# Cross-attention without the loop over pairs, with the product of probabilities and values taken for four tiles at a time

## What is computed

```python
q = proj(norm(x), Wq, bq); k = proj(context, Wk, bk); v = proj(context, Wv, bv)
scores = clip(einsum('bhsd,bhtd->bhst', q, k) / 4, -50, 50)
scores = clip(where(attend, scores, -10000.0), -50, 50)
probs = softmax(scores); probs = probs / (probs.sum(-1) + 1e-08)
ctx = einsum('bhst,bhtd->bhsd', probs, v)
delta = clip(residual_scale, 0, 0.3) * (ctx @ Wo.T + bo)
x = x + layernorm(delta) * ln_gamma + ln_beta
```

## Time and profile before

| what | value |
|---|---|
| median of 3 runs | 1797.5 us (1793.64 to 1798.63) |
| profiled execution, its own time | 1795.94 us |
| its span, first to last instruction | 1794.1 us |
| PE busy | 1594.6 us, 89% |
| PE weight loads busy | 1341.1 us, 75% |
| DVE busy | 1454.5 us, 81% |
| ACT busy | 1117.9 us, 62% |
| POOL busy | 734.8 us, 41% |
| granted PE clock, mean | 0.946 |

### The profile page before, as it was taken

One profiled execution on the slowest core, in us unless ns is written; L12 is line 12 of the kernel. 1 busy time (PEld: TensorE's weight loads), 2 busy tenths in 40 slices (PEclk: granted clock), 3 DMA queues, 4 the chain that ended last, 5 costly groups with the idle time before them and its releaser, 6 DMA issues. The chain is left out here.

```text
span 1794.1 us, 48379 instructions
## 1 busy us (share of the span) xinstructions
PE 1594.6 (89%) x18290; PEld 1341.1 (75%) x18290; DVE 1454.5 (81%) x2513; ACT 1117.9 (62%) x2155; POOL 734.8 (41%) x743
## 2 busy tenths in 40 slices
PE   5899999998739999999999999999999999999464
PEld 5888888886528878787887787877877878788233
DVE  3788877875467898888888988888889888898698
ACT  3566555664337776676676666766766667677463
POOL 1565555553163443443343434433434344343133
PEclk9999999998769999999999999999999999999678
DMA  6000000000221111111111111111111111110001
GB/s 183 1 1 2 2 1 1 1 0 1 85 79 47 48 48 39 45 47 48 36 47 48 47 42 42 47 48 37 47 48 48 46 38 47 48 47 2 1 11 31
DMA packets 41611, 66.85 MB, mean 37 GB/s; under 512 B 7749, under 2 KB 40194, under 8 KB 41282
## 3 DMA queue, kind: packets, MB, share of 16 engines
q1 hardware_dynamic: 41410, 63.93, 12.3%
HBM read 62.08 MB, written 1.84 MB: 36 GB/s over the span
## 5 line engine op out<-in xcount | busy, mean ns | idle before, releaser
L1146 POOL TENSOR_TENSOR xa_CW<-xa_CTX,xa_CH 128x500 fp32r<-128x500 f32 x187 | 283.1, 1514 | 676.6 <-ACT xa_CH L1337 674.3
L1365 DVE TENSOR_TENSOR xl_ACC<-xl_ACC,xl_PB 125x896 f32<-125x896 f32 x320 | 422.0, 1319 | 36.1
L1329 ACT ACTIVATE xl_PB<-banks,xl_BIB,xl_SCB 125x896 f32<-125x896 f32 x384 | 400.8, 1094 | 74.5 <-PE banks L1203 74.5
L1356 DVE TENSOR_SCALAR xl_PB<-xl_PB 125x896 f32<-125x896 f32 x384 | 269.9, 703 | 57.2 <-ACT xl_PB L1329 53.6
L1311 ACT ACTIVATE xl_V<-banks 125x256 f32<-125x256 f32 x384 | 147.5, 384 | 179.6 <-PE banks L1170 179.6
L1170 PE MATMUL banks<-xa_WVhigh,xa_CH 128*125 128x256 f32 x768 | 239.5, 312 | 0.0
L1170 PE MATMUL banks<-xa_WVlow,xa_CH 128*125 128x256 f32 x768 | 217.0, 283 | 0.0
L1170 PE MATMUL banks<-xa_WVhigh,xa_CW 128*125 128x256 f32 x768 | 216.1, 281 | 0.0
L1219 PE MATMUL banks<-xl_PB,xl_V 125*32 125x112 f32 x6144 | 199.8, 271 | 2.5 <-DVE xl_PB L1356 1.7
L1302 ACT ACTIVATE xl_KXhigh<-banks,xa_bk 128x500 fp32r<-128x500 f32 x192 | 130.3, 679 | 104.2 <-PE banks L1170 104.2
L1170 PE MATMUL banks<-xa_CH,xa_WKhigh 128*128 128x500 f32 x384 | 152.5, 397 | 33.8 <-POOL xl_ONES L1108 27.7
(11 more groups left out here) (235 smaller groups left out, 4074.5 us busy)
## 6 DMA issues: line engine op xcount, KB each, us to landing
xa_CTX<-in_ctxT SPq DMA_DIRECT2D x93, 500.0 KB, 3.6
fw_WO<-in_W_o SPq DMA_DIRECT2D x1, 2048.0 KB, 17.7
xq_WR<-in_w_gating SPq DMA_DIRECT2D x1, 2048.0 KB, 9.5
X<-in_x SPq DMA_DIRECT2D x1, 1792.0 KB, 10.1
out<-ff_R SPq DMA_DIRECT2D x16, 112.0 KB, 1.9
fw_QUT<-in_W_quT SPq DMA_DIRECT2D x1, 1536.0 KB, 12.3
xa_CTX<-in_ctxT SPq DMA_DIRECT2D x1, 1500.0 KB, 14.8
xq_WL<-in_w_linear SPq DMA_DIRECT2D x1, 1024.0 KB, 11.7
```

The costliest lines, as they stand in the source:

```text
L1146: nc.gpsimd.tensor_tensor(context_piece(CW, i), context_piece(CTX, i), context_piece(CH, i), ALU.subtract).then_inc(ctx_low, 1)
L1329: nc.scalar.activation(PB[t % PR][:, :, :], banks[0:TK, 2 * i:2 * i + KT, 0:QW], ACT.Exp, scale=SCB[j][:, t:t + 1], bias=BIB[j][:, t:t + 1 ...
L1356: nc.vector.tensor_scalar(pt, pt, E_HI, E_LO, ALU.min, ALU.max).then_inc(clipped, 1)
L1365: nc.vector.tensor_tensor(ACC[j][:, :, :], prev[:, :, :], PB[t % PR][:, :, :], ALU.add).then_inc(summed, 1)
```

## The change

- `pairs` writes the body of a pair 16 times; no engine has the loop any more.
- PV is done only at odd u of the step before, so in even steps, for the four tiles of the two steps before; `pv_done` counts once per two steps, and the waits on it are divided by two. The buffers of the probabilities and of V become six each.
- In step 3 the projection stands between the two tiles of V, not before both.
- The three POOL operations of `add_delta` go to steps 6, 8 and 9, and its last self-wait is dropped; the fourth step of the normalization goes from step 7 to 6, and ACT's logarithm and exponential for it from step 6 to 5.

```diff
--- before.py
+++ after.py
@@ -58,7 +58,7 @@
 XD = H // NH
 HPT = P // XD
 QW = HPT * S
-PR = 4
+PR = 6
 MADE = 5
 CLIP = 50.0
 E_HI, E_LO = float(np.exp(np.float64(CLIP))), float(np.exp(np.float64(-CLIP)))
@@ -1032,7 +1032,7 @@
     ALL = B * STEPS
     AC = TILES - 1
     K_AHEAD, C_AHEAD = 3, MADE
-    PROJECT, NORM = 3, {4: (0, 1), 5: (2,), 7: (3,), 10: (4, 5), 11: (6,)}
+    PROJECT, NORM, ADD_DELTA = 3, {4: (0, 1), 5: (2,), 6: (3,), 10: (4, 5), 11: (6,)}, (6, 8, 9)
     with ExitStack() as stack:
         sb, sem = tools(nc, stack, "xl")
         KX = [sb(f"KX{part}", [P, KT, CL], F32R) for part in ("high", "low")]
@@ -1075,10 +1075,8 @@
 
         def pairs(eng, body):
 
-            body(0, True, False)
-            with eng.Fori(1, PAIRS - 1) as g:
-                body(g, False, False)
-            body(PAIRS - 1, False, True)
+            for g in range(PAIRS):
+                body(g, g == 0, g == PAIRS - 1)
 
         def half_rows(half):
             return slice(half * 64, (half + 1) * 64)
@@ -1108,16 +1106,18 @@
                 nc.gpsimd.memset(ONES[:, :], 1.0).then_inc(ones_ready, 1)
                 pool.wait_ge(ones_ready, 1)
 
-                def add_delta(g):
-
-                    pool.wait_ge(dn_ready, g + 1)
-                    nc.gpsimd.tensor_tensor(DL[:, :], DL[:, :], GAM[:, :], ALU.mult).then_inc(affine, 1)
-                    pool.wait_ge(affine, g * 2 + 1)
-                    nc.gpsimd.tensor_tensor(DL[:, :], DL[:, :], BET[:, :], ALU.add).then_inc(affine, 1)
-                    pool.wait_ge(affine, g * 2 + 2)
-                    xg = X[:, bass.ds(g, 1), :]
-                    nc.gpsimd.tensor_tensor(xg, xg, DL[:, :].unsqueeze(1), ALU.add).then_inc(x_added, 1)
-                    pool.wait_ge(x_added, g + 1)
+                def add_delta(g, step):
+
+                    if step == 0:
+                        pool.wait_ge(dn_ready, g + 1)
+                        nc.gpsimd.tensor_tensor(DL[:, :], DL[:, :], GAM[:, :], ALU.mult).then_inc(affine, 1)
+                    elif step == 1:
+                        pool.wait_ge(affine, g * 2 + 1)
+                        nc.gpsimd.tensor_tensor(DL[:, :], DL[:, :], BET[:, :], ALU.add).then_inc(affine, 1)
+                    else:
+                        pool.wait_ge(affine, g * 2 + 2)
+                        xg = X[:, bass.ds(g, 1), :]
+                        nc.gpsimd.tensor_tensor(xg, xg, DL[:, :].unsqueeze(1), ALU.add).then_inc(x_added, 1)
 
                 def spread_queries(g, j, b):
 
@@ -1153,12 +1153,13 @@
                                 if not (first and j == 0):
                                     pool.wait_ge(exp_done, b * TILES)
                                 mask_columns(ng, nj, b + 1)
-                        if s == 8 and not first:
-                            add_delta(g - 1)
+                        if s in ADD_DELTA and not first:
+                            add_delta(g - 1, ADD_DELTA.index(s))
                 spread_queries(0, 0, 0)
                 mask_columns(0, 0, 0)
                 pairs(pool, pair)
-                add_delta(PAIRS - 1)
+                for step in range(len(ADD_DELTA)):
+                    add_delta(PAIRS - 1, step)
 
             @block.tensor
             def _(pe):
@@ -1179,9 +1180,9 @@
                     split_products(bank[K_BANK][:, 0:CK], lambda a, kt: WK[a][:, kt, m * P:(m + 1) * P],
                                    lambda a, kt: ctx_parts[a][:, kt, c * CK:(c + 1) * CK]).then_inc(k_done, 1)
 
-                def values(n, u, early=False):
-
-                    for i in range(2):
+                def values(n, u, tiles, early=False):
+
+                    for i in tiles:
                         t = 2 * u + i
                         if not early:
                             pe.wait_ge(v_ready, n * 2 + i - 1)
@@ -1211,7 +1212,7 @@
                 def values_product(n, u):
 
                     pe.wait_ge(v_ready, n * 2 + 2)
-                    for i in range(2):
+                    for i in range(-2, 2):
                         t = 2 * u + i
                         pe.wait_ge(clipped, n * 2 + i + 1)
                         for kt in range(KT):
@@ -1251,18 +1252,21 @@
                         scores(n, j, u, first and s == 0)
                         if not (first and s == 0):
                             pu = (u - 1) % STEPS
-                            if pu == 0 and not (first and j == 0):
+                            if pu == 1 and not (first and j == 0):
 
                                 pe.wait_ge(d_read, b)
-                            values_product(n - 1, pu)
+                            if pu % 2 == 1:
+                                values_product(n - 1, pu)
                             if pu == STEPS - 1:
                                 denominators(b - 1, 1 - j)
+                        if more(last, s, 1):
+                            values(n + 1, (u + 1) % STEPS, (0,))
                         if s == PROJECT and not first:
 
                             pe.wait_ge(k_ready, n + K_AHEAD)
                             project(g - 1)
                         if more(last, s, 1):
-                            values(n + 1, (u + 1) % STEPS)
+                            values(n + 1, (u + 1) % STEPS, (1,))
                         if more(last, s, K_AHEAD):
 
                             pe.wait_ge(k_ready, n + K_AHEAD)
@@ -1279,7 +1283,7 @@
                         pe.wait_ge(k_ready, p)
                     keys(p, p)
                     if p == 1:
-                        values(0, 0, early=True)
+                        values(0, 0, (0, 1), early=True)
                 pairs(pe, pair)
                 values_product(ALL - 1, STEPS - 1)
                 denominators(B - 1, 1)
@@ -1302,10 +1306,10 @@
                     nc.scalar.activation(KX[0][:, m, c * CK:(c + 1) * CK], bank[K_BANK][:, 0:CK], ACT.Identity,
                                          bias=bk[:, m:m + 1]).then_inc(kh_ready, 1)
 
-                def values_out(n, u, early=False):
-
-                    if not early:
-                        act.wait_ge(pv_done, n - 1)
+                def values_out(n, u):
+
+                    if n >= 3:
+                        act.wait_ge(pv_done, (n - 1) // 2)
                     for i in range(2):
                         act.wait_ge(v_done, n * 2 + i + 1)
                         nc.scalar.activation(V[(2 * u + i) % PR][:, :], bank[V_BANK[i]][0:TK, 0:H], ACT.Copy).then_inc(v_ready, 1)
@@ -1320,8 +1324,8 @@
                         for i in range(2):
                             t = 2 * u + i
                             act.wait_ge(s_done, n * 2 + i + 1)
-                            if not (first and s < 2):
-                                act.wait_ge(pv_done, n - 1)
+                            if n >= PR // 2:
+                                act.wait_ge(pv_done, (n - 1) // 2)
                                 if t >= PR:
                                     act.wait_ge(summed, b * AC + max(1, t - PR))
                                 else:
@@ -1329,7 +1333,7 @@
                             nc.scalar.activation(PB[t % PR][:, :, :], banks[0:TK, 2 * i:2 * i + KT, 0:QW], ACT.Exp,
                                                  scale=SCB[j][:, t:t + 1], bias=BIB[j][:, t:t + 1]).then_inc(exp_done, 1)
                         if more(last, s, 1):
-                            values_out(n + 1, (u + 1) % STEPS, first and s == 0)
+                            values_out(n + 1, (u + 1) % STEPS)
                         if more(last, s, C_AHEAD):
                             i = (s + C_AHEAD) % STEPS
                             if i % KT == 0:
@@ -1337,13 +1341,13 @@
                             nc.scalar.activation(context_piece(CH, i), context_piece(CTX, i), ACT.Copy).then_inc(ctx_high, 1)
                         if more(last, s, K_AHEAD):
                             keys_high(n + K_AHEAD, (s + K_AHEAD) % STEPS)
-                        if s == 6 and not first:
+                        if s == 5 and not first:
                             delta_rstd(g - 1)
                 nc.scalar.preload_act_table_set("natural_log_exp_and_others")
                 for p in range(K_AHEAD):
                     keys_high(p, p)
                     if p == 1:
-                        values_out(0, 0, early=True)
+                        values_out(0, 0)
                 pairs(act, pair)
                 delta_rstd(PAIRS - 1)
 
@@ -1378,7 +1382,7 @@
                 def read_output(b):
 
                     src = by_head(0)
-                    dve.wait_ge(pv_done, b * STEPS + STEPS)
+                    dve.wait_ge(pv_done, (b * STEPS + STEPS) // 2)
                     dve.wait_ge(den_done, b + 1)
                     nc.vector.tensor_scalar(OM[:, :, :], src[:, :, 0, :], D2[:, 0:1], None, ALU.mult).then_inc(o_half, 1)
                     dve.wait_ge(o_half, b + 1)
```

## The result

The changed kernel takes 1736.7 us (median of 4 runs, 1733.1 to 1737.9) against 1796.6 for the kernel before: a ratio of 0.9665, 95% interval 0.9645 to 0.9685. The forecast was 1723, its range 1702 to 1750. The profiled execution took 1733.1 us, 62.8 less than the one of before. 3.8 of that lie ahead of the first key product of `cross_loop` (523.0 against 526.8), in stages that the change does not touch: the K of step 0 of pair 0 came between 536.5 (after) and 541.8 (e10_light) in the profiled executions, at 541.2 before, 540.3 in e1_straight and 538.3 in e4_no_moves. From that K to the last one of the stage it is 1110.45 us before and 1053.77 after, so the pairs themselves gave 56.7 of the 62.8.

The account below looks back on a forecast made before the run. PE was taken to bound cross-attention, DVE close behind. Four stretches, 6.45 + 16.8 + 17.0 + 26.1 = 66.35 us a pair against 71.56, gave -70.7, first and last pair -3.4: 1723 us, range 1702 to 1750.

Parts of the forecast that it names:

- 3.7: Loop's back edge on PE: 2.15 us of gap before the scores plus 1.55 of slow clock, at 13 edges.
- B: Stretch from step 11's key products to those of the next pair's step 0: 6.45 us, from 9.50.
- 999.6: Cross-attention pairs before the change: 14 × 71.56 us less one edge's 2.2.
- Product every second step: PE's product of probabilities and values: one leaving of the column groups fewer, 0.20 us per two steps.
- D: Stretch from step 3's key products to step 6's: two long steps, one short, denominators; 17.0 us, 0.5 more than before.
- C: Stretch from step 0's key products to step 3's: set by DVE, its delta reading ending last; 16.8 us, from 17.82.
- rival 2: GpSimd gets more in DVE's way: 1.65 us more lost in two DVE-set stretches, pair 68.0, time 1746; chance 0.21.
- A: Stretch from step 6's key products to step 11's: set by DVE, 26.1 us, from 27.72; PE alone 25.45.
- Residual's moves: Steps 6 to 11: normalization and first GpSimd product move to step 6, each taking 0.3 us off DVE's work.
- PE alone: Rival: PE alone sets the pair, DVE's order hinders nothing; pair 64.7 us, time 1700; chance 0.10.
- Code loading: Rival: loading straight code stalls PE, 3.7 us a stall; two a pair give 1828 us; chance 0.03.
- The gap between pairs: Rival: the gap is not the loop's and stays; 13 × 2.85 = 37 us lost, time 1760; chance 0.04.

Follow-up runs that it names:

- e10_light: The changed kernel with DVE's clip of each second tile over half of its columns only: 1719.5 us, ratio 0.9584.
- e1_straight: The kernel before with its 16 pairs as straight code and nothing else changed: 1734.1 us, ratio 0.9663.
- e4_no_moves: The changed kernel with the projection, add_delta, the normalization's fourth step and ScalarE's part back in their old places: 1755.2 us, ratio 0.9783.
- e3_no_pv: The changed kernel with the product of probabilities and values in every step again and four buffers: 1722.9 us, ratio 0.9598.
- e9_unroll2: The kernel before with two pairs in each loop trip, so 6 back edges in place of 13: 1776.7 us, ratio 0.9899.
- e7_projection: e1_straight with only the projection moved between the two tiles of V: 1730.0 us, ratio 0.9638.
- e5_read_early: e3_no_pv with DVE's reading of the projection in step 3 put ahead of the add: 1719.6 us, ratio 0.9586.
- e8_residual: e1_straight with only the residual's moves (add_delta's three operations, the normalization's fourth step, ScalarE's part): 1727.2 us, ratio 0.9630.
- e12_pool_half: The changed kernel with GpSimd's subtraction for the context's low part over half of its columns from pair 1 on: 1713.6 us, ratio 0.9549.
- e6_pv_split: The changed kernel with the values product for step 2's tiles done in step 3 and for step 3's in step 4: 1724.6 us, ratio 0.9611.
- e2_pv_loop: The kernel before, loop kept, with the values product every second step and six buffers, nothing else: 1840.7 us, ratio 1.0254.

## Why the prediction was right, and where it was wrong

The mechanism that carries the gain was forecast and is shown: the back edges go, and with them their idle time, the lower clock and 0.1 us at each add. The size is less good than the time looks. The pairs gave 56.7 us where 74.1 were forecast: 60.0 by straight code (before to e1_straight), 10.0 by the moves (to e3_no_pv), less 13.4 for the product every second step (to the changed kernel); some 6 us more came in the profiled execution from stages that the change does not touch, which is luck.

- *Straight code takes the gap and the slow stretch.* Right: e1_straight, and in part e9_unroll2. The 3.7 was the edge by itself; net it is 3.1 in the kernel before, since a pair without an edge waits 0.69 for DVE instead. In the new kernel the long even step covers that lateness, so that B came out as forecast. The sum takes 2.2 off for the entry of the loop where its own price is 3.7; the first pair of the loop is in fact 3.6 shorter (67.97), but the other thirteen are 71.67 on the mean and not 71.56, so the 999.6 is right by luck (999.7).
- *0.1 at each add on DVE.* The rows bear it out, and it is worth more than a side remark: by the working above 19 of the 60 us, as far as that part is due to these waits. A rule that DVE's time is free because PE bounds the stage would have missed it.
- *Product every second step: 0.20 less per two steps.* This step failed. PE saves 0.13 (6.15 + 4.46 against 2 × 5.37), the four tiles taking 1.67 and not 1.60. But the part was booked as a gain in the first and last pair, its cost in B and D was never set against a kernel without it, and it is a loss of 13.8 us. The first pair gave 1.5 (59.51 to 58.01) and the last lost 0.35 (51.23 to 51.58), where -3.4 was forecast for both. The working had the ingredients, D 0.5 longer, and C set by DVE whatever PE has to do there. It compared the new kernel with the old one only, never with the new one without this part; then it would have shown that C's shorter step 3 is worth nothing and D's and B's longer ones cost. "1.0 is what C gains in all" is 0.54 in truth, 0.35 of it straight code's (e1_straight) and 0.19 the projection's (e7_projection).
- *C 16.8.* Off by 0.5. The order of events was right, the reading of the projection ends last (e5_read_early). The four adds of steps 1 and 2 took 1.09, 2.04, 1.09 and 2.05, where the loop had 1.09, 1.09, 1.61 and 1.96: 0.52 more, the collisions of rival 2, in small.
- *A 26.1.* 26.4; DVE's order and its waits at steps 9 and 11 as forecast (e10_light), 0.3 too small; which instructions of DVE hold the 0.3 was not looked for.
- *B and D*: off by 0.09 and 0.15, the 0.07 by which the product of four tiles was too short.
- *Residual's moves 0.3 and 0.3 in A.* They gave 0.25 in A and 0.23 in B in e8_residual, but 0.97 in A beside the product every second step (e4_no_moves).
- *Rivals.* PE alone: excluded by the waits; its A is reached only when work is left out, on DVE or GpSimd (25.67 in e10_light and e12_pool_half, against the 25.45 of the sum). GpSimd in DVE's way: the mechanism is real (e12_pool_half). Of the 1.02 between 66.35 and 67.37, C and A hold 0.78, less than half of the 1.65 foreseen, and only the 0.5 in C is traced to such adds; B and D hold the other 0.24, which is PE's four-tile product. Code loading: no gap by issue of over 0.5 us in the straight pairs. The gap between pairs: gone. (The 2.85 a pair of that rival is worked out nowhere; by the prediction's own terms the gap is 2.15, and 3.7 with the clock.)
- *Signs.* Clock 1.00, 0.35 before the scores and adds 0.03 to 0.04 behind their clips came as told. Three did not: the pair is 67.4 and not 66 to 67; DVE is busy 91% of the stage and not over 92; PE waits 1.2 us in step 3 as told, but 0.2 and not a us at K of step 9. All four waits sum to 1.9, well under the 4 of rival 2. (The 99% that PE was said to read in the slices can't be read there, a 9 being 90% or more; by the earlier trace rows it is 95%, 68.31 of 71.6.)

What stays open: why pair 5 alone is 1.2 us longer after and in e6_pv_split. DVE and GpSimd take turns in another order in it: in step 6 the subtraction starts 0.08 ahead of the add, which then takes 2.15, and in pair 6 0.28 behind it, where the add takes 1.09 and the subtraction 1.96. K of step 9 waits 1.45 for DVE in pair 5 and 0.20 to 0.22 in the others. What tips the order was not looked for. Open too: why the slow part behind a back edge is 3.4 us in one loop and 6.8 in another.

The rule of the Trainium skill on the shared ports ("SBUF — State Buffer", SBUF: two separate sides) holds for a DVE operation with two inputs in SBUF, as the add, beside a GpSimd operation that reads SBUF, as the subtraction: the one that starts first holds the ports for the whole instruction. The add of 2.04, which ends 0.94 behind the subtraction, agrees with it. Halving the subtraction was worth 23 us here (e12_pool_half).

## What to carry to other kernels

Price each part of a change against the kernel that has all the others, not only against the old one: here one part gave 60 us and hid another that cost 14. Work that lies beside a wait is free where it stands; before it is batched or moved, look whether the place it goes to has a wait as well. An engine that is busy 91% of the time and shares a resource can set the time through one hand-over late in its step, and the cheapest cure is the order of its own instructions.

## What the runs showed of the hardware

- A back edge of the loop, with 924 products and as many weight loads in its body, costs PE 2.1 to 2.5 us more idle time than the usual 0.35 and then 3.4 us at the lower level of the clock (0.50 from 888.80 to 892.20), at each of the 13 edges; in e2_pv_loop, and at two of the six edges of e9_unroll2, it is 6.8 us. An edge cost 3.1 us net in the kernel before and up to 6 in the others. Work that falls in such a stretch is dearer: the four-tile product took 2.80 us there and 1.47 elsewhere.
- Straight code of 16 bodies moved no more over the instruction queues than 3 bodies with a loop: 2.77 MB against 2.93. No gap by issue of over 0.5 us came with it.
- DVE's add starts 0.12 to 0.14 us behind its clip in the loop, where its waits compare with numbers worked out from g, and 0.03 to 0.04 in straight code.
- An add on DVE took 2.04 to 2.15 us beside a GpSimd subtraction that had started before it, and 1.09 alone.
- After a product on the column groups PE's weight loads pause for 0.17 us; halving the number of times was worth 0.13 us per two steps, 1% of them.
